# Scores of fifteen batches by seven block products in place of eight, in a transformer block on one core

## The chip, the cores and the metric

One of the eight cores of a Trainium2 chip runs the whole kernel. The metric is the device time of one execution in microseconds (us), the median of three runs. A profiled execution of its own gives the trace: for each engine every instruction with its start and length, and who released it. TensorE does the matmuls, VectorE (DVE), ScalarE (ACT) and GpSimd (POOL) the element work, SyncE (SP) issues nearly all transfers. A "bank" is one of the eight banks of PSUM (512 columns of float32 on 128 partitions).

## The reference

Sixteen batches of 1024 rows with 256 columns go through attention and a gated feed-forward part:

```python
def attn(t, W_qkv, b_qkv):
    qkv = jnp.einsum('bnd,ed->bne', t, W_qkv) + b_qkv
    Q, K, V = qkv[:, :, :256], qkv[:, :, 256:512], qkv[:, :, 512:]
    scores = jnp.einsum('bqd,bkd->bqk', Q, K) / jnp.sqrt(jnp.float32(256))
    return jnp.einsum('bqk,bkv->bqv', jax.nn.softmax(scores, axis=-1), V)

def ffn(x, w_gate, w_up, w_down):        # int32 weights times 1/127, hidden size 768
    gate = jnp.einsum('bsd,hd->bsh', x, wg)
    up = jnp.einsum('bsd,hd->bsh', x, wu)
    return jnp.einsum('bsh,dh->bsd', jax.nn.silu(gate) * up, wd)

x = x + layernorm(attn(layernorm(x), W_qkv, b_qkv))
x = x + layernorm(ffn(layernorm(x), w_gate, w_up, w_down))
```

## The kernel before

Every float32 operand of a matmul is split into a high and a low half of 16 bits (names ending in h and l), and a product a x b is three matmuls: high x high, high x low, low x high (`pairs`, `passes`, line 710). A batch has eight tiles of 128 rows; `g` is the half of four tiles, `b` the batch.

The steps of a batch. `x_stats`, `x_norm`, `x_hat`, `x_high` and `x_low` normalise x into `xs` and split it into `xh`, `xl`; `turn_x` transposes these by DMA into `xTh`, `xTl`. `project_z` multiplies with the folded matrix A = Wq'Wk, so that the scores are z times x transposed; `z_high` (ScalarE), `z_float` (VectorE) and `z_low` (GpSimd) split z from PSUM. `score(b, i)` makes the 128 x 1024 scores of query tile i in two banks: per bank 2 x 3 matmuls of 512 columns, one group of three for each half `dj` of the 256 columns that are summed over. `row_max` (L613, L617) takes the row maximum and makes the bias `nmx`, `exp` (L438) makes P, which frees the two banks; `p_high` and `p_low` split P, `turn_p` transposes it. `attend(b, g, u)` multiplies P with x (12 matmuls of 512 columns; four of them per half `g`, two for each output half `dh`), `o_high` and `o_low` split the result, `project_v` applies V (24 matmuls of 256 columns). `y_scale`, `y_stats`, `y_norm`, `x1_add` make the first residual in `X[k]`, `x1_norm`, `y_hat`, `y_high`, `y_low`, `turn_y` its normalised transposed halves `yTh`, `yTl`. `gate_up(b, g, c)` makes one of six hidden chunks of gate and up in two banks (8 matmuls of 512 columns, since the low half of the integer weights is zero here), `silu` (L473), `h_mul` (L679), `h_high` (L480) and `h_low` (L374) make its halves, `down` (24 matmuls of 256 columns) the output, `d_stats`, `d_norm`, `d_add`, `add_bias` the second residual, and `store` writes it. `reload` loads x a second time into one of four slots of `X`.

Nothing schedules this at run time. The order on each engine is written out by hand: a start-up part, a loop over the batches (on TensorE from b = 1 to 12), and the last batches. A wait is a semaphore and a count (`wait_ge`); a `gate_up` or `score` names in its call the semaphores that say its two banks are free. On TensorE a pass of the loop is: attends of batch b with scores of b + 1 between them, then the twelve `gate_up` of batch b, with `project_z` of b + 2 and the `down` of b - 1 and b between them. `attend` of batch b uses the banks 6 and 7, `project_v` and `down` 4 and 5, scores 0 to 3, and gates and z take 0 to 3, 6 and 7 in turn.

## Time and the profile before

| | |
|---|---|
| median of 3 runs | 1382.4 us (1381.77 to 1383.32) |
| the profiled execution | 1381.28 us, its span from first to last instruction 1379.5 us |
| TensorE busy | 1347.5 us (98%), 7332 matmuls |
| VectorE, ScalarE, GpSimd busy | 897.7, 879.5, 826.1 us |
| mean granted clock | 0.997 of full speed |

The page of the profile lists busy time by engine, the span in 40 slices, the DMA queues, the chain that ended last and the costliest groups. Matmuls overlap in the array, so their mean length (380 ns for 512 columns) is longer than the distance from one to the next.

### The profile page before, as it was taken

What the parts mean: (1) busy time and instruction counts of PE and PEld (TensorE: products, weight loads), DVE (VectorE), ACT (ScalarE), POOL (GpSimd) and SP (SyncE); (2) the same over time, 40 slices, a digit from 0 to 9 for tenths busy, and PEclk for the clock granted to TensorE, in tenths of its full rate; (3) what the DMA queues carried; (4) which work ended last, traced back from release to release, by engine and by line L of the source; (5) the groups of instructions that cost most, each with busy time, mean ns of one, the idle gap of its engine ahead of it and who ended that gap; (6) DMA issues with size and microseconds to landing.
All of it is one profiled execution on the core that took longest, in us unless ns stands there. A gap on an engine that the chain in (4) does not pass through costs nothing.

```text
span 1379.5 us, 22219 instructions
## 1 busy us (share of the span) xinstructions
PE 1347.5 (98%) x7332; PEld 721.1 (52%) x7332; DVE 897.7 (65%) x2160; ACT 879.5 (64%) x1373; POOL 826.1 (60%) x1002
## 2 busy tenths in 40 slices
PE   6898999999999999999999999999999999999987
PEld 3353555554555545555554555545555555555544
DVE  5875666666657667666666656667566666657565
ACT  4757575675766567575775757567575774756544
POOL 1768376484746748376484755748376484745544
PEclk9999999999999999999999999999999999999999
DMA  6997382653827457383653736547373664716311
GB/s 191 175 186 166 55 160 68 138 133 69 161 77 130 115 96 141 88 154 73 134 142 69 161 78 122 123 92 146 79 151 85 121 135 82 136 56 121 92 36 51
DMA packets 437175, 158.27 MB, mean 115 GB/s; under 512 B 418113, under 2 KB 420417, under 8 KB 437058
## 3 DMA queue, kind: packets, MB, share of 16 engines
q1 hardware_dynamic: 436272, 156.03, 54.5%
q8 instruction: 60, 0.98, 0.3%
q10 hardware_dynamic: 786, 0.79, 0.2%
q14 instruction: 57, 0.47, 0.1%
HBM read 36.70 MB, written 16.78 MB: 39 GB/s over the span
## 4 chain that ended last, share of the span: by engine, by line
PE 94%; DVE 3%; issue 1%; DMA 1%; POOL 1%; ACT 0%; ACTq 0%; POOLq 0%
PE S L710 93%; DMA hTh<-in_L_attn_W_qkv 1%; DVE mxs L613 0%; DVE S L642 0%; DVE st L651 0%; POOL rs L293 0%; PE S L736 0%; DMA yTl<-yl 0%; DVE st L669 0%; DVE X L664 0%; DVE hf L679 0%; DVE zw L606 0%; POOL yl L365 0%; DVE xl L320 0%; ACT yn L458 0%
## 5 line engine op out<-in xcount | busy, mean ns | idle before, releaser
L438 ACT ACTIVATE P<-S,nmx,sc 128x1024 f32<-128x1024 f32 x128 | 154.0, 1203 | 282.5 <-DVE nmx L617 282.5
L613 DVE TENSOR_REDUCE mxs<-S 128x1 f32<-128x1024 f32 x128 | 156.2, 1220 | 125.0 <-PE S L710 124.7
L679 DVE SCALAR_TENSOR_TENSOR hf<-S,sc,hf 128x512 f32<-128x512 f32 x192 | 142.0, 746 | 140.1 <-ACT hf L473 134.3
L338 POOL TENSOR_TENSOR Pl<-P,Ph 128x1024 f16<-128x1024 f32 x96 | 206.0, 2147 | 33.9 <-issue 26.4
L710 PE MATMUL S<-xTh,zTh 128*128 128x512 f16 x512 | 194.6, 380 | 4.4 <-ACT P L438 2.2
L710 PE MATMUL S<-PTh,xh 128*128 128x512 f16 x512 | 194.0, 379 | 1.0 <-DVE hf L679 1.0
L710 PE MATMUL S<-xTh,zTl 128*128 128x512 f16 x512 | 194.8, 380 | 0.0
L710 PE MATMUL S<-xTl,zTh 128*128 128x512 f16 x512 | 194.7, 380 | 0.0
L710 PE MATMUL S<-PTl,xh 128*128 128x512 f16 x512 | 194.0, 379 | 0.0
L710 PE MATMUL S<-PTh,xl 128*128 128x512 f16 x512 | 194.0, 379 | 0.0
L289 POOL TENSOR_SCALAR rs<-mv,sc 128x2 f32<-128x2 f32 (+1 forms) x96 | 35.3, 368 | 230.7 <-DVE mv L655 191.3
L710 PE MATMUL S<-Wh,hTh 128*128 128x256 f16 x768 | 170.4, 273 | 1.9 <-DVE X L703 1.7
L374 POOL TENSOR_TENSOR hTl<-hf,hTh 128x512 f16<-128x512 f32 x128 | 146.3, 1157 | 41.1 <-ACT hTh L480 36.8
L710 PE MATMUL S<-Wh,hTl 128*128 128x256 f16 x768 | 170.4, 273 | 0.0
L473 ACT ACTIVATE hf<-S,sc 128x512 f32<-128x512 f32 x192 | 130.9, 683 | 54.2 <-POOL hTl L374 35.6
L293 POOL TENSOR_TENSOR rs<-rs,mhalf 128x4 f32<-128x4 f32 (+1 forms) x160 | 145.2, 907 | 13.3
L710 PE MATMUL S<-yTh,Gh 128*128 128x512 f16 x384 | 146.1, 380 | 5.3 <-DMA yTl<-yl 3.9
L710 PE MATMUL S<-yTl,Gh 128*128 128x512 f16 x384 | 146.0, 380 | 0.0
L710 PE MATMUL S<-yTh,Uh 128*128 128x512 f16 x384 | 146.0, 380 | 0.0
L710 PE MATMUL S<-yTl,Uh 128*128 128x512 f16 x384 | 146.0, 380 | 0.0
L480 ACT ACTIVATE hTh<-hf 128x512 f16<-128x512 f32 x192 | 120.0, 625 | 34.3 <-DVE hf L679 34.3
L445 ACT ACTIVATE Ph<-P 128x1024 f16<-128x1024 f32 x128 | 135.3, 1057 | 5.2 <-DMA PTl<-Pl 1.7
(113 smaller groups left out, 2462.2 us busy)
## 6 DMA issues: line engine op xcount, KB each, us to landing
xs<-in_L_attn_t SPq DMA_DIRECT2D x32, 512.0 KB, 5.3
X<-in_L_attn_t SPq DMA_DIRECT2D x32, 512.0 KB, 4.6
out_x<-X SPq DMA_DIRECT2D x64, 256.0 KB, 2.9
PTh<-Ph SPq DMA_TRANSPOSE x128, 3.2
PTl<-Pl SPq DMA_TRANSPOSE x128, 3.3
hTh<-in_L_attn_W_qkv ACTq DMA_DIRECT2D x1, 768.0 KB, 7.2
hTl<-in_L_ffn_w_gate SPq DMA_DIRECT2D x1, 768.0 KB, 7.2
hTh<-in_L_ffn_w_up SPq DMA_DIRECT2D x1, 768.0 KB, 9.0
```

Of the source, the lines that this page charges most:

```text
L289: p.engine.tensor_scalar(rs, var, scalar1=eps, scalar2=mul, op0=ALU.add, **({} if mul is None else {"op1": ALU.mult})).then_inc(g_step, 1)
L293: return p.engine.tensor_tensor(out=rs, in0=rs, in1=mhalf[:, 0:rs.shape[1]], op=ALU.pow)
L338: p.engine.tensor_tensor(out=Pl[:, m % 3, :], in0=P[:, m % 2, :], in1=Ph[:, m % 3, :], op=ALU.subtract).then_inc(pl_vector if i in PL_ON_V ...
L374: p.engine.tensor_tensor(out=hTl[g][:, c, :], in0=hf[:, n % 3, :], in1=hTh[g][:, c, :], op=ALU.subtract).then_inc(hl_vector if c in HL_ON_ ...
L438: a.engine.activation(P[:, m % 2, :], ps[:, bank:bank + 2, :].rearrange("p a n -> p (a n)"), ACT.Exp, bias=nmx[:, c:c + 1], scale=sS, accu ...
L445: a.engine.activation(Ph[:, m % 3, :], P[:, m % 2, :], ACT.Copy).then_inc(ph_done, 1)
L473: a.engine.activation(hf[:, n % 3, :], ps[:, bank, :], ACT.Silu, scale=sc2[:, 3:4]).then_inc(silu_done, 1)
L480: a.engine.activation(hTh[g][:, c, :], hf[:, n % 3, :], ACT.Copy).then_inc(hh_done, 1)
L613: v.engine.tensor_reduce(mxs[:, c:c + 1], ps[:, bank:bank + 2, :].rearrange("p a n -> p (a n)"), axis=AX.X, op=ALU.max, negate=True).then_ ...
L679: v.engine.scalar_tensor_tensor(out=hf[:, n % 3, :], in0=ps[:, bank + 1, :], scalar=sc2[:, 4:5], in1=hf[:, n % 3, :], op0=ALU.mult, op1=AL ...
L710: done = t.engine.matmul(out, s, m, start=(start and i == 0), stop=(stop and i == len(terms) - 1))
```

## The change

The scores of batch 0 stay as they are. For batches 1 to 15 the product z x' is cut in blocks, two by two by two: the rows of z into even and odd tiles (a pair j of tiles 2j and 2j + 1), the 256 summed columns into two halves, the keys into two halves. With z blocks A11, A12 (even tile), A21, A22 (odd tile) and x blocks B, sums on both sides are formed first (S1 to S4 of z in `z_mix`, T1 to T4 of x in `x_mix`, in place in `xs`), split into halves and, for x, transposed (`T_high`, `T_low`, `turn_T`). Seven products P1 to P7 and sums of them give the four blocks C11, C12 (even tile), C21, C22 (odd tile). Some of the sums are made by accumulating a product onto one that lies in the bank (P5 and then P3 onto P1 in bank 1, P7 and then P4 onto P6 in bank 2), others by VectorE with a copy of the earlier state that ScalarE took (`s1`, `s6`, `s15`). The VectorE sum also yields the maximum, which takes the place of `row_max`.

The order on all engines is new. In a pass of the loop on TensorE the `gate_up` of the second half of batch b - 1 and the first half of batch b follow the attention of batch b, so gates run half a batch later than before, and `project_z` and the scores of b + 2 (pairs 0 and 1) stand in the same pass. `X` has three slots in place of four. Scale constants change to leave room for the sums, the float staging buffer `ft` goes, and the three loads of feed-forward weights are issued earlier.

```diff
-        X = two("X", [128, 4, D], f32, 4)
+        X = two("X", [128, 4, D], f32, 3)
+        Th, Tl = two("Th", [128, 4, D]), two("Tl", [128, 4, D])
+        TTh, TTl = sb("TTh", [128, NT, 2, 128], f16), sb("TTl", [128, NT, 2, 128], f16)
+        s1, s6, s15 = sb("s1", [128, 512]), sb("s6", [128, 512]), sb("s15", [128, 512])
...
+        def T_high(a, b, g):
+            a.wait_ge(xm_done, 4 * (b - 1) + 4 - g)
+            a.wait_ge(T_turned[g], 32 * (b - 1))
+            a.engine.activation(Th[g][:, :, :], xs[:, 4 * g:4 * g + 4, :], ACT.Copy).then_inc(Th_done, 1)
...
+        def zm_high(a, b, g):
+            n, js = 2 * (b - 1) + g, slice(2 * g, 2 * g + 2)
+            z_used(a, b - 1, g)
+            for k in range(2):
+                a.wait_ge(zm_done, 4 * n + 2 * k + 2)
+                a.engine.activation(zTh[:, 3 + 2 * k:5 + 2 * k, js, :], zs[:, 2 * k:2 * k + 2, :, :], ACT.Copy).then_inc(zmh_done, 1)
+
+        def copy_P1(a, b, j):
+            n = 4 * (b - 1) + j
+            a.wait_ge(P1_done, n + 1)
+            a.wait_ge(C11_done, n)
+            a.wait_ge(C21_done, n)
+            a.engine.activation(s1[:, :], ps[:, 1, :], ACT.Copy).then_inc(s1_done, 1)
...
+        def x_mix(v, b, part):
+
+            xl_wait(v, b, 0)
+            xl_wait(v, b, 1)
+            x00, x01, x10, x11 = (xs[:, 4 * g:4 * g + 4, 128 * d:128 * d + 128] for g in range(2) for d in range(2))
+            for k, (out, x, y) in enumerate(((x00, x10, x00), (x10, x11, x10), (x11, x11, x00), (x01, x01, x11))):
+                if k // 2 == part:
+                    v.wait_ge(xm_done, 4 * (b - 1) + k)
+                    v.engine.tensor_tensor(out=out, in0=x, in1=y, op=ALU.subtract).then_inc(xm_done, 1)
...
+        def z_mix(v, b, g):
...
+            v.engine.tensor_tensor(out=S3, in0=A11, in1=A21, op=ALU.subtract).then_inc(zm_done, 1)
+            v.engine.tensor_tensor(out=S1, in0=A21, in1=A22, op=ALU.add).then_inc(zm_done, 1)
+            v.wait_ge(zm_done, 4 * n + 2)
+            v.engine.tensor_tensor(out=S2, in0=S1, in1=A11, op=ALU.subtract).then_inc(zm_done, 1)
+            v.wait_ge(zm_done, 4 * n + 3)
+            v.engine.tensor_tensor(out=S4, in0=A12, in1=S2, op=ALU.subtract).then_inc(zm_done, 1)
+
+        def add_max(v, out, a, s, seed, top):
+            return v.engine.tensor_tensor_reduce(out=out, in0=a, in1=s, scale=1.0, scalar=seed, op0=ALU.add, op1=ALU.max,
+                                                 accum_out=top)
...
+        def join_C22(v, b, j):
+            n = 4 * (b - 1) + j
+            v.wait_ge(P7_done, n + 1)
+            v.wait_ge(s15_done, n + 1)
+            add_max(v, ps[:, 3, :], ps[:, 2, :], s15[:, :], LOWEST, mxs[:, n % 2, 2:3]).then_inc(C22_done, 1)
+
+        def join_C12(v, b, j):
+            n = 4 * (b - 1) + j
+            v.wait_ge(P3_done, n + 1)
+            v.wait_ge(s6_done, n + 1)
+            v.wait_ge(C11_done, n + 1)
+            add_max(v, ps[:, 1, :], ps[:, 1, :], s6[:, :], mxs[:, n % 2, 0:1], mxs[:, n % 2, 1:2]).then_inc(C12_done, 1)
+            v.wait_ge(C12_done, n + 1)
+            nmx_of(v, 8 * b + 2 * j, mxs[:, n % 2, 1:2])
...
+        def product(t, bank, j, k, moving, start):
+            mh, ml = moving
+            done = None
+            for i, (s_, m) in enumerate(pairs((zTh[:, k, j, :], zTl[:, k, j, :], mh, ml))):
+                done = t.engine.matmul(cols(ps[:, bank, :]), s_, m, start=(start and i == 0), stop=(i == 2),
+                                       skip_group_check=not start)
+            return done
...
+        def score_first(t, b, j, free0, free1, free2, free3):
...
+            t.wait_ge(*free1)
+            product(t, 1, j, 0, x_block(b, 0, 0), True).then_inc(P1_done, 1)
+            t.wait_ge(*free2)
+            product(t, 2, j, 5, T_block(1, 1), True).then_inc(P6_done, 1)
+            t.wait_ge(*free0)
+            product(t, 0, j, 1, x_block(b, 0, 1), True).then_inc(P2_done, 1)
+            t.wait_ge(s1_done, n + 1)
+            product(t, 1, j, 4, T_block(0, 0), False).then_inc(P5_done, 1)
+            t.wait_ge(s6_done, n + 1)
+            t.wait_ge(*free3)
+            product(t, 2, j, 3, T_block(1, 0), False).then_inc(P7_done, 1)
+
+        def score_second(t, b, j):
+            n = 4 * (b - 1) + j
+            t.wait_ge(s15_done, n + 1)
+            product(t, 1, j, 6, x_block(b, 1, 1), False).then_inc(P3_done, 1)
+            t.wait_ge(C22_done, n + 1)
+            product(t, 2, j, 2, T_block(0, 1), False).then_inc(P4_done, 1)
...
+            for b in range(1, 14):
                 attend(t, b, 0, 1)
+                score_first(t, b + 1, 2, (exp_done, 8 * b + 11), (exp_done, 8 * b + 11), (exp_done, 8 * b + 12), (exp_done, 8 * b + 12))
                 project_v(t, b, 0, (ft_done[0], 4 * b - 2), (ft_done[1], 4 * b - 2))
                 attend(t, b, 1, 2, (ol_done[1], 2 * b + 1))
                 attend(t, b, 1, 3)
+                score_second(t, b + 1, 2)
                 attend(t, b, 1, 0, (ol_done[0], 2 * b + 1))
                 attend(t, b, 1, 1)
+                score_first(t, b + 1, 3, (exp_done, 8 * b + 13), (exp_done, 8 * b + 13), (exp_done, 8 * b + 14), (exp_done, 8 * b + 14))
+                score_second(t, b + 1, 3)
                 project_v(t, b, 1, (x1_done, 8 * b + 2), (x1_done, 8 * b + 4))
+                gate_up(t, b - 1, 1, 0, 6, (ol_done[0], 2 * b + 2), (ol_done[1], 2 * b + 2), three)
+                gate_up(t, b - 1, 1, 1, 0, (exp_done, 8 * b + 15), (exp_done, 8 * b + 15), three)
+                project_z(t, b + 2, 0, 2, (exp_done, 8 * b + 16), (exp_done, 8 * b + 16))
...
+                project_z(t, b + 2, 1, 0, (silu_done, 12 * b + 4), (hmul_done, 12 * b + 4))
+                attend(t, b + 1, 0, 2, (hmul_done, 12 * b + 6))
+                score_first(t, b + 2, 0, (zw_done, 4 * b + 11), (zw_done, 4 * b + 12), (silu_done, 12 * b + 5), (hmul_done, 12 * b + 5))
                 down(t, b, 0, 0, (ft_done[0], 4 * b), three)
+                score_second(t, b + 2, 0)
                 down(t, b, 0, 1, (ft_done[1], 4 * b), three)
+                attend(t, b + 1, 0, 3)
+                score_first(t, b + 2, 1, (exp_done, 8 * b + 17), (exp_done, 8 * b + 17), (exp_done, 8 * b + 18), (exp_done, 8 * b + 18))
+                score_second(t, b + 2, 1)
+                attend(t, b + 1, 0, 0, (silu_done, 12 * b + 6))
```

In the elided stretch of the loop stand the other ten `gate_up` (four more of batch b - 1, six of batch b) and the two `down(b - 1, 1, ...)`, the first of them behind eight `gate_up` and one `project_z`. VectorE's order around a pair j = 1 or 3 is `join_C11`, `o_low`, `join_C22`, `join_C12`, `join_C21`; for batch 15 the attends of each half are followed at once by `project_v`.

## Rows read from the trace of the kernel before

**Rows 1.** The page's first part: busy us, share of the span, instructions.

```profile
PE 1347.5 (98%) x7332; PEld 721.1 (52%) x7332; DVE 897.7 (65%) x2160; ACT 879.5 (64%) x1373; POOL 826.1 (60%) x1002
```

**Rows 2.** The chain that ended last, in order: start us, length us, what.

```profile
119.73 1150.22 PE S L710 x6312
```

**Rows 3.** Timeline of TensorE: start us, length us, engine, line, operation.

```profile
122.22 0.38 PE L710 MATMUL S<-yTl,Gh 128*128 128x512 f16 x1
122.44 0.38 PE L710 MATMUL S<-yTh,Uh 128*128 128x512 f16 x1
...
137.98 0.27 PE L710 MATMUL S<-Wh,hTh 128*128 128x256 f16 x1
138.09 0.27 PE L710 MATMUL S<-Wh,hTl 128*128 128x256 f16 x1
```

**Rows 4.** One batch: PE, PEld, DVE, ACT, POOL busy; clock, DMA share, GB/s.

```profile
460.00:543.00 83.00, 83.00 (x458) 44.57 (x457) 54.61 (x133) 54.56 (x87) 51.51 (x63) 1.00 0.59 115
```

**Rows 5.** Groups by line and shape: busy us, mean ns, idle us before and releasers.

```profile
L613 DVE TENSOR_REDUCE mxs<-S 128x1 f32<-128x1024 f32 x128 | 156.2, 1220 | 125.0 <-PE S L710 124.7 <-issue 0.3
L438 ACT ACTIVATE P<-S,nmx,sc 128x1024 f32<-128x1024 f32 x128 | 154.0, 1203 | 282.5 <-DVE nmx L617 282.5
L374 POOL TENSOR_TENSOR hTl<-hf,hTh 128x512 f16<-128x512 f32 x128 | 146.3, 1157 | 41.1 <-ACT hTh L480 36.8 <-DVE hf L679 4.3
...
L679 DVE SCALAR_TENSOR_TENSOR hf<-S,sc,hf 128x512 f32<-128x512 f32 x192 | 142.0, 746 | 140.1 <-ACT hf L473 134.3 <-PE S L710 5.7
L445 ACT ACTIVATE Ph<-P 128x1024 f16<-128x1024 f32 x128 | 135.3, 1057 | 5.2 <-DMA PTl<-Pl 1.7
L473 ACT ACTIVATE hf<-S,sc 128x512 f32<-128x512 f32 x192 | 130.9, 683 | 54.2 <-POOL hTl L374 35.6 <-PE S L710 18.2
...
L328 POOL TENSOR_TENSOR zTl<-zw,zTh 128x512 f16<-128x512 f32 x60 | 80.9, 1368 | 1.2 <-PE S L710 1.2
...
L320 POOL TENSOR_TENSOR xl<-xs,xh 128x1024 f16<-128x1024 f32 x30 | 63.8, 2127 | 0.0
...
L651 DVE BATCH_NORM_STATS2 st<-S 128x6 f32<-128x256 f32 x128 | 47.9, 416 | 0.0
...
L630 DVE SCALAR_TENSOR_TENSOR oTl<-S,oTh 128x512 f16<-128x512 f32 x64 | 44.0, 688 | 58.2 <-ACT oTh L451 57.9
...
L451 ACT ACTIVATE oTh<-S 128x512 f16<-128x512 f32 x64 | 37.5, 586 | 55.0 <-PE S L710 55.0
...
L438 ACT ACTIVATION_READ_ACCUMULATOR P<-S,nmx,sc 128x1 f32 x128 | 24.6, 192 | 0.0
```

**Rows 6.** The chain again, from 27 to 39 us: reader after TensorE, TensorE after writer.

```profile
27.85 2.76 PE S L710 x12
...
30.63 1.24 DVE mxs L613
...
35.34 0.75 DVE zw L606
...
36.14 2.76 PE S L710 x12
```

**Rows 7.** Timeline of TensorE around its stalls; in brackets idle time and releaser.

```profile
106.00 0.39 PE L710 MATMUL S<-xTh,zTh 128*128 128x512 f16 x1 [2.19 <-ACT P L438]
...
108.50 0.63 PE L710 MATMUL S<-xTh,zTl 128*128 128x512 f16 x1
108.92 0.63 PE L710 MATMUL S<-xTh,zTh 128*128 128x512 f16 x1
...
1280.51 0.38 PE L710 MATMUL S<-PTh,xh 128*128 128x512 f16 x1 [0.98 <-DVE hf L679]
...
1332.28 0.59 PE L710 MATMUL S<-yTh,Gh 128*128 128x512 f16 x1 [3.93 <-DMA yTl<-yl]
```

**Rows 8.** DMA from 40 to 60 us: queue share, and transposes' time to landing.

```profile
q1 hardware_dynamic: 11824, 3.91, 95.4%
...
xTl<-xl SPq DMA_TRANSPOSE x2, 3.2
```

More of the change, by code:

```diff
@@ new lines, in _ @@
+            copy_P15(a, 15, 1)
+            p_high(a, 15, 1)
+            y_hat(a, 13, 1, 0)
+            exp(a, 15, 2, 0)
+            y_hat(a, 13, 1, 1)
+            exp(a, 15, 3, 2)
+            p_high(a, 15, 2)
+            o_high(a, 14, 0, 0)
+            copy_P1(a, 15, 2)
+            copy_P6(a, 15, 2)
+            y_high(a, 13, 1)
+            copy_P15(a, 15, 2)
+            add_bias(a, 13, 0, 0)
+            p_high(a, 15, 3)
+            add_bias(a, 13, 0, 1)
+            o_high(a, 14, 1, 1)
@@ new lines, in _ @@
+            exp(a, 15, 4, 0)
+            exp(a, 15, 5, 2)
+            p_high(a, 15, 4)
+            p_high(a, 15, 5)
+            copy_P1(a, 15, 3)
+            copy_P6(a, 15, 3)
+            o_high(a, 14, 1, 0)
+            copy_P15(a, 15, 3)
+            y_hat(a, 14, 0, 0)
+            y_hat(a, 14, 0, 1)
+            exp(a, 15, 6, 0)
+            exp(a, 15, 7, 2)
+            y_high(a, 14, 0)
+            silu(a, 13, 1, 0, 6)
+            silu(a, 13, 1, 1, 0)
+            silu(a, 13, 1, 2, 2)
@@ L1397, in _ @@
-            y_high(a, 14, 0)
-            o_high(a, 14, 1, 1)
-            exp(a, 15, 5, 2)
-            p_high(a, 15, 5)
-            exp(a, 15, 6, 0)
-            p_high(a, 15, 6)
             silu(a, 14, 0, 0, 6)
```

1764 lines of the change are left out of this document (976 added, 788 removed).

## The prediction

> **What bounds the kernel now.** I read the page first: TensorE is busy 98% of the span, the other three compute engines 60 to 65% [rows 1]. Busy matmuls overlap, so the share alone proves little; the chain of waits, in order of time, does. From 119.7 us it holds nothing but matmuls for 1150.2 us [rows 2]. The timeline then gives what a matmul costs in that stretch: one of 512 columns starts 0.216 us after the one before it, one of 256 columns 0.109 us [rows 3]. Counting the source, the kernel has 4,992 of the first kind and 2,304 of the second behind the set-up: 1077.3 + 251.4 = 1328.7 us of the 1379.5. So the middle is a TensorE stream without a hole, and the 51 us left lie ahead of the first product, in the stalls before 121 us, and in the last 110 us. A matmul taken from the middle is worth its 0.216 us, as long as no other engine is then too slow. The view of equal stretches shows one batch as 83.0 us, with VectorE at 54.6, ScalarE 54.6 and GpSimd 51.5, at full granted clock [rows 4].
>
> **Removed.** Scores take eight block products per pair of query tiles; batches 1 to 15 now take seven. A product is three matmuls of 512 columns; 15 batches x 4 pairs x 3 = 180 matmuls fewer, 180 x 0.216 = **38.8 us** off the stream. Nothing else on TensorE changes in count (512-column products have the same shape as now).
>
> **Added to the others, per batch.** VectorE loses eight row maxima (1.22 us each) and gets sixteen joins. No row shows a join (add two tensors, keep the maximum). Nearest is the 512-column operation with one operand in PSUM, 0.75 us; 0.69 is the lowest of that size, 1.22 (a reduction of 1024 columns) what it would be at half the rate. I take 0.75, since it does the same reads. Eight sums of 256 columns in z_mix (0.42, as the statistics of 256 columns; at most 0.69) and four of 512 in x_mix (0.69, as o_low, the shortest row of 512 columns with two tensors; at most twice that, since here both operands lie in SBUF and no row has both in float32). 54.6 - 9.8 + 12.0 + 3.4 + 2.8 = 63.0 us. ScalarE: twelve copies out of PSUM at 0.59, two T_high at 1.06, four zm_high of 512 columns at 0.68, z_high in six pieces of about 0.5 for four of 0.68 (an estimate from the 512-column row: half the columns, most of the fixed part): 54.6 + 7.1 + 2.1 + 2.7 + 0.3 = 66.8. GpSimd: two T_low at 2.13, four zm_low at 1.37, z_low in smaller pieces (about -1.3): 60.0 [rows 4, 5]. All are under the 81 us that TensorE will want, so each addition costs nothing by its sum; what counts is order and latency. The four turn_T per batch land in 3.2 us like other transposes, and the queues are half empty in the middle [rows 4, 8].
>
> **The new chain inside a pair of tiles.** TensorE now waits for copies of its own results. A group of twelve starts at 27.85 and its reader at 30.63; 12 x 0.216 = 2.59 is the group's share of the stream, so a reader starts 0.19 us after a product's share has passed. z_float ends at 36.09 and TensorE goes on at 36.14, 0.05 us after a writer [rows 6]. Count from P1's start, with a product 0.65: P6, P2, P5 and P7 start at 0.65, 1.29, 1.94, 2.59. The copy of P1 ends at 0.65 + 0.19 + 0.59 = 1.43, before 1.94; the copy of P6 before 2.59. P5's copy ends at 2.59 + 0.19 + 0.59 = 3.37, and P3 could have started at 3.24: 0.18 lost. C22 starts when P7 is visible (3.43), ends at 4.18, and P4 could have started at 4.07: 0.16 lost. VectorE has o_low (0.69) between C11 and C22 in both such pairs, which puts C22 about 0.15 later: **0.5 us a pair** where score_second stands right behind score_first. That is so for j = 1 and j = 3, two pairs in each of 15 batches: 15.0 us. Bounds: 0.34 each (10 us), and with joins of 1.22 us 0.5 + 0.47 (29 us). For j = 0 a down product (24 x 0.109 = 2.6 us) stands between, for j = 2 a project_v and two attends (7.8 us); those hide the chain. The bank releases are covered too: the exp of both tiles ends some 3.5 us behind P4 (0.19, a join, a bias of some 0.2, two exps of 1.2 and a read of 0.19), and two 12-matmul groups (5.2 us) stand between a pair and the next.
>
> One tight place more: P1 of j = 0 goes into a bank that z_float has to free. After project_z: 0.19, a third of z_high, z_float, z_high, z_float = 2.5 us, behind an attend of 2.59. And ScalarE's copy of P1 there stands behind add_bias, which waits for d_add behind z_float: ready at about 4.55 where P5 wants it at 4.53. I give 0.25 us a batch to both, 3.5 us in 14 batches; without the cover of that attend it would be 2.5 us a batch.
>
> The accumulator deserves a doubt. On ScalarE a result kept beside an output is a second instruction of 0.19 us [rows 5]. The Trainium skill (VectorE: DVE Perf Modes, section on two Vector instructions with no wait between them) counts a VectorE operation that also writes its accumulator as two instructions; the trace before has no such VectorE operation. If the read costs what ScalarE's does, each immediate pair loses 0.19 more, 5.7 us in all; I leave it out of the sum and inside the range.
>
> **Start.** Now the stream loses, up to 119.7 us, 2.35 us for an exp (a gap of 2.19 and a start late), 1.7 us because the clock is granted at half (1.2 of 2.4 GHz) for eight matmuls (0.42 us apart where 0.216 is full rate), 0.3, and 1.45 for a bank that z_float frees, which ends where the long stretch begins: 5.8 us [rows 2, 7]. After the change gate_up(0,0,0) needs y of the first half. Counted from P1 of the last pair of batch 1, ScalarE has: copies to 3.4, x_high and p_high 2.1, four y_hat 2.1, an exp with its read 1.4, y_high 1.06; GpSimd y_low 2.13; the transpose 3.2: 15.4 us. TensorE has the pair (5.0), project_v 2.6, project_z 2.6: 10.2. It stalls 5.2 us, and the clock falls as it did after the gap of 2.19 us: 1.7 more. z_low of batch 0 in three pieces costs 0.6. Together 7.5, so **+1.7 us**.
>
> **End.** The gap of 3.93 us for y goes (six gate_up of batch 14 and more now stand ahead), with its half clock, 4.08 + 1.7, and 1.14 us around a gap of 0.98: 6.9. But project_v(15, g) now follows the last attend at once: 0.19 + 0.59 + 0.69 + 0.05 = 1.5 us for o_high and o_low, twice: 3.0. **-3.9 us** [rows 5, 7]. The stall before the last down stays.
>
> **Gates half a batch later; three slots of X.** The order matters where gates release banks. Count from the start of gate_up(b-1,1,0). GpSimd waits for y_stats (3.7 us by the four y_scale and eight statistics operations of 0.42 and less), then y_norm 1.8 (four small operations), y_low 2.1, two h_low 2.3, x_low 2.1, z_low 2.1, two h_low 2.3: 16.4. down(b-1,1,0) stands behind eight gate_up (1.73 each) and a project_z, at 16.4, and needs chunks 3 to 5 at 17.0. That is 0.6 us of margin, so I cost it at nothing, though narrowly. The third X slot is reloaded behind stores that end a dozen microseconds before x1_add asks: nothing.
>
> **Sum.** 1379.5 - 38.8 + 15.0 + 3.5 + 1.7 - 3.9 = 1357.0 us of span. The profiled execution took 1381.28, 1.8 more than its span; the median of the runs, 1382.4, is another 1.1 above: 1359.9, say **1360 us**.
>
> **Rivals.** (A) Joins at half rate: an immediate pair loses 0.47 more (14 us) and, with its accumulator, up to 0.66 (20 us), while VectorE's batch grows by 16 x 0.66 to 73.5 us and its order begins to bind, say 0.5 us a batch (7 us): with 18 us for the pairs 1385 us. For it: no such row; against: every 512-column row with a PSUM operand takes 0.69 to 0.75. By the Trainium skill (Vector Engine (DVE) Microarchitecture Reference, section 7) a scalar-tensor-tensor with two SBUF sources that are not bf16 halves its throughput for want of a port for the accumulator; here one source is in PSUM, and h_mul's row with the same sources is not halved.
> (B) The other side: the gates' half binds. One mechanism, GpSimd's h_low of chunk 4 in front of down(b-1,1,0). The margin is 0.6 us; each microsecond beyond it costs one per batch. The gain left above, 22.5 us, is gone at 1.6 us a batch, so GpSimd 2.2 us later than counted decides. At 3 us late the time is 1360 + 14 x 2.4 = 1394 us. For it: nine operations in a row, counted without any wait for ScalarE's halves, and silu waits for hTl already, 35.6 us in all [rows 5]; against: the middle today has no hole.
> (C) The chain is hidden: shorter latencies, stalls half as long, and no y stall at the start: 1345 us.
> (D) The start is bound by transposes: from 40 to 60 us the queues are 95% busy [rows 8], and turn_T adds four of 1.3 us and batch 1's need comes earlier: up to 10 us, 1370 us.
>
> **Numbers.** Forecast 0.56 (its own range 1350 to 1368), A 0.10, B 0.10, C 0.12, D 0.12. This kernel's measurement can tell about 0.2%, 2.8 us. Faster by more: forecast, C, D and a little of A and B, 0.82; within it 0.04; slower 0.14. The range 1346 to 1383 leaves out the lower half of C and most of A and B.
>
> **What would show it.** TensorE with 7,152 matmuls; between 121 and 1270 us holes of 0.1 to 0.3 us ahead of P3 (released by ScalarE's copy) and P4 (by the join), two of each per batch, and no half clock; a join at 0.75 us; the first gate waiting for yTl; no wait of 3.9 us at the end. I am wrong if joins take over 1 us, if TensorE waits for hTl or hf in the gates, or if holes exceed 1.5 us a batch.

## The result and the profile after

The changed kernel took 1486.99 us (median of four runs, 1486.27 to 1487.63) where the kernel before took 1382.09 (1381.41 to 1383.32): a ratio of 1.0758, 95% interval 1.0743 to 1.0772. It is 105 us slower; 1360 was forecast, 22 us faster. Both the sign and the size were wrong, and the range missed by 104 us.

First the page's busy times, which answer to [rows 1]:

```profile
PE 1355.5 (91%) x7152; PEld 705.2 (47%) x7152; DVE 1180.7 (79%) x2703; ACT 1047.1 (70%) x1683; POOL 978.4 (66%) x1084
```

The 180 matmuls are gone, as foretold, but TensorE is no longer busy throughout. The page's chain that ended last, by engine and by line, had been one stretch of matmuls for 1150 us [rows 2]:

```profile
PE 56%; DVE 24%; issue 10%; POOL 3%; ACT 3%; DMA 2%; SPq 2%; DVEq 0%; ACTq 0%; POOLq 0%
PE S L854 45%; PE S L935 11%; DVE zs L708 3%; DVE hTl L419 3%; DVE zs L710 2%; DVE hf L823 2%; DVE xs L688 2%; DVE zs L707 2%; DMA xTl<-xl 2%; SPq L277 1%; DVE st L674 1%; DVE S L715 1%; DVE zw L698 1%; DVE X L847 1%; POOL Tl L353 1%
```

A quarter of it is VectorE, at the lines of z_mix (zs), x_mix (xs), its own h_low (hTl) and h_mul (hf). The joins (S L715) are 1%. One batch, from one project_z to that of the next batch, in the columns of [rows 4]:

```profile
206.90:296.40 89.50, 83.72 (x446) 43.50 (x444) 73.56 (x171) 66.22 (x108) 62.59 (x69) 0.98 0.58 118
```

89.5 us where 80.4 would be the bare stream (83.0 less 12 matmuls). ScalarE is at 66.2 (66.8 forecast), GpSimd at 62.6 (60.0), but VectorE at 73.6 where 63.0 was forecast. The groups by line and shape say which of its operations (columns as in [rows 5]; L707 to L712 are z_mix, L688 x_mix, L419 h_low, L715 the joins, here those with a seed, and the read of their accumulator):

```profile
L715 DVE CUSTOM_DVE_ANT_0 S<-S,s,mxs 128x512 f32<-128x512 f32 x120 | 90.5, 754 | 1.1 <-PE S L935 0.6
...
L688 DVE TENSOR_TENSOR xs<-xs 128x512 f32<-128x512 f32 x60 | 75.9, 1265 | 2.4 <-POOL xl L346 1.4
L419 DVE TENSOR_TENSOR hTl<-hf,hTh 128x512 f16<-128x512 f32 x64 | 74.8, 1168 | 9.0 <-ACT hTh L559 8.6
...
L712 DVE TENSOR_TENSOR zs<-zw,zs 128x256 f32<-128x256 f32 x30 | 47.9, 1598 | 1.0
...
L708 DVE TENSOR_TENSOR zs<-zw 128x256 f32<-128x256 f32 x30 | 46.6, 1552 | 0.0
...
L710 DVE TENSOR_TENSOR zs<-zs,zw 128x256 f32<-128x256 f32 x30 | 36.1, 1202 | 1.0
...
L715 DVE DVE_READ_ACCUMULATOR2_ANT mxs<- 128x1 f32 x240 | 34.0, 142 | 0.0
...
L707 DVE TENSOR_TENSOR zs<-zw 128x256 f32<-128x256 f32 x30 | 25.7, 856 | 0.1
```

A z_mix operation was priced at 0.42 us and takes 1.30 on average (156.3 us for 120), an x_mix operation 1.27 for 0.69. Shapes alone can't explain 0.86 beside 1.60 us for the same 256 columns. The timeline of VectorE over some microseconds of a batch, and below it GpSimd's, can:

```profile
212.20 0.50 DVE L707 TENSOR_TENSOR zs<-zw 128x256 f32<-128x256 f32 x1
212.63 1.38 DVE L708 TENSOR_TENSOR zs<-zw 128x256 f32<-128x256 f32 x1
214.04 2.24 DVE L710 TENSOR_TENSOR zs<-zs,zw 128x256 f32<-128x256 f32 x1
216.31 1.26 DVE L712 TENSOR_TENSOR zs<-zw,zs 128x256 f32<-128x256 f32 x1
...
218.57 2.06 DVE L823 SCALAR_TENSOR_TENSOR hf<-S,sc,hf 128x512 f32<-128x512 f32 x3
220.55 2.83 DVE L688 TENSOR_TENSOR xs<-xs 128x512 f32<-128x512 f32 x2
```

GpSimd's:

```profile
211.26 2.45 POOL L419 TENSOR_TENSOR hTl<-hf,hTh 128x512 f16<-128x512 f32 x2
213.68 2.31 POOL L346 TENSOR_TENSOR xl<-xs,xh 128x1024 f16<-128x1024 f32 x1
215.95 1.34 POOL L361 TENSOR_TENSOR zTl<-zw,zTh 128x512 f16<-128x512 f32 x1
```

Read the ends: L710 ends at 216.28, just behind GpSimd's xl (215.99); L708 at 214.01, just behind GpSimd's second hTl (213.71); L712 at 217.57, behind zTl (217.29). One VectorE operation of two SBUF sources ends a moment after each GpSimd operation ends, however short it would be by itself. The h_mul between them, which have a source in PSUM, did not lengthen: 742 ns on average over all 192, 746 before [rows 5].

What TensorE makes of it, in its timeline of the same batch:

```profile
219.36 0.39 PE L854 MATMUL S<-yTh,Uh 128*128 128x512 f16 x1 [1.91 <-DVE hf L823]
...
225.09 0.27 PE L854 MATMUL S<-Wh,hTh 128*128 128x256 f16 x1 [2.30 <-DVE hTl L419]
...
226.26 0.42 PE L854 MATMUL S<-Wh,hTh 128*128 128x256 f16 x1
226.47 0.42 PE L854 MATMUL S<-Wh,hTl 128*128 128x256 f16 x1
...
251.41 0.39 PE L935 MATMUL S<-TTh,zTh 128*128 128x512 f16 x1 [1.12 <-DVE mxs L715]
...
260.30 0.38 PE L935 MATMUL S<-TTh,zTl 128*128 128x512 f16 x1
260.72 0.39 PE L935 MATMUL S<-xTh,zTh 128*128 128x512 f16 x1
```

The wait of 1.91 us is for a bank that h_mul frees, behind z_mix in VectorE's order; the 2.30 us are for down's hTl, behind x_mix; then the clock is granted at half (matmuls of 256 columns 0.21 us apart from 225.6 to 228.4, 0.11 at full rate [rows 3]), 1.7 us; the 1.12 us are for C22, since z_mix of the second half ended late in front of the joins. The half clock is no accident of this batch: between 150 us and the last project_z it is granted in 13 stretches, and what the matmuls there lose by starting at twice their distance adds up to some 20 us of the middle. At 260 us stands the first of the two holes that were forecast in a pair: 0.42 us between starts where 0.22 is the stream, 0.20 ahead of P3; the one ahead of P4 is 0.24.

All of TensorE in one table: the distances of its matmuls' starts less 0.216 us for 512 columns and 0.109 for 256, added up. "Start" runs from the first project_z to 150 us, "middle" to the last project_z (13 batches in the changed kernels), "end" to the last matmul.

```
                      first z    start   middle    end
before                19.7 us     14.6      0.3    9.3
after                 21.3        41.2    117.5    8.7
```

1.6 + 26.6 + 117.2 - 0.6 - 38.8 = 106.0 us; the spans differ by 106.3.

### The profile page after: what moved, and what is told of

Same layout as the page of the kernel before. It is cut to its first block, busy times and chain, and to the rows that moved or that the text cites. A ratio compares the mean times of both kernels' runs of the same rounds, so it can differ in the third digit from the quotient of the medians.

```text
span 1485.8 us, 23358 instructions
## 1 busy us (share of the span) xinstructions
PE 1355.5 (91%) x7152; PEld 705.2 (47%) x7152; DVE 1180.7 (79%) x2703; ACT 1047.1 (70%) x1683; POOL 978.4 (66%) x1084
## 4 chain that ended last, share of the span: by engine, by line
PE 56%; DVE 24%; issue 10%; POOL 3%; ACT 3%; DMA 2%; SPq 2%; DVEq 0%; ACTq 0%; POOLq 0%
PE S L854 45%; PE S L935 11%; DVE zs L708 3%; DVE hTl L419 3%; DVE zs L710 2%; DVE hf L823 2%; DVE xs L688 2%; DVE zs L707 2%; DMA xTl<-xl 2%; SPq L277 1%; DVE st L674 1%; DVE S L715 1%; DVE zw L698 1%; DVE X L847 1%; POOL Tl L353 1%
## 5 line engine op out<-in xcount | busy, mean ns | idle before, releaser
L854 PE MATMUL S<-Wh,hTh 128*128 128x256 f16 x768 | 189.5, 290 | 33.5 <-DVE hTl L419 31.7
L419 POOL TENSOR_TENSOR hTl<-hf,hTh 128x512 f16<-128x512 f32 x128 | 159.9, 1269 | 73.9 <-ACT hTh L559 38.3
L854 PE MATMUL S<-Wh,hTl 128*128 128x256 f16 x768 | 189.5, 290 | 0.0
L823 DVE SCALAR_TENSOR_TENSOR hf<-S,sc,hf 128x512 f32<-128x512 f32 x192 | 137.6, 742 | 24.0 <-PE S L854 14.4
L715 DVE CUSTOM_DVE_ANT_0 S<-S,s 128x512 f32<-128x512 f32 x120 | 83.9, 700 | 55.6 <-PE S L935 41.5
L935 PE MATMUL S<-TTh,zTh 128*128 128x512 f16 x240 | 91.9, 383 | 17.4 <-DVE mxs L715 14.9
L321 POOL TENSOR_SCALAR rs<-mv,sc 128x2 f32<-128x2 f32 (+1 forms) x96 | 29.0, 302 | 118.2 <-DVE mv L795 90.3
L854 PEld LDWEIGHTS S<-Wh,hTh 128*128 128x128 f16 x768 | 79.5, 104 | 57.0 <-issue 34.9
L321 POOL TENSOR_SCALAR rs<-mv 128x4 f32<-128x4 f32 x64 | 25.5, 398 | 117.6 <-DVE mv L817 82.7
```

The costliest lines, as they stand in the source:

```text
L321: p.engine.tensor_scalar(rs, var, scalar1=eps, scalar2=mul, op0=ALU.add, **({} if mul is None else {"op1": ALU.mult})).then_inc(g_step, 1)
L419: p.engine.tensor_tensor(out=hTl[g][:, c, :], in0=hf[:, n % 3, :], in1=hTh[g][:, c, :], op=ALU.subtract).then_inc(hl_vector if c in HL_ON_ ...
L715: return v.engine.tensor_tensor_reduce(out=out, in0=a, in1=s, scale=1.0, scalar=seed, op0=ALU.add, op1=ALU.max, accum_out=top)
L823: v.engine.scalar_tensor_tensor(out=hf[:, n % 3, :], in0=ps[:, bank + 1, :], scalar=sc2[:, 4:5], in1=hf[:, n % 3, :], op0=ALU.mult, op1=AL ...
L854: done = t.engine.matmul(out, s, m, start=(start and i == 0), stop=(stop and i == len(terms) - 1))
L935: done = t.engine.matmul(cols(ps[:, bank, :]), s_, m, start=(start and i == 0), stop=(i == 2), skip_group_check=not start)
```

## The experiments

Each kernel is the changed one with the edit shown, but for the two ports programs. Where one run is named, there is one timed execution and no interval; elsewhere the median of four runs is given, with the ratio to the kernel before and its 95% interval in brackets. Middle and start are counted as in the table above.

### Is it the sums' form, or GpSimd beside them?

**ports.** A program of its own, which does none of the kernel's work: VectorE does eight operations of each kind, each waiting for the last, first alone, then while GpSimd subtracts 1024 columns without pause.

```diff
+ for n in range(70): p.tensor_tensor(out=pc[n % 4][:, :], in0=pa[:, :], in1=pb[:, :], op=ALU.subtract)
+ for _ in range(8): step(v.tensor_tensor(out=ra[:, 0:256], in0=u[:, 0:256], in1=w[:, 0:256], op=ALU.subtract))
```

> A kernel of its own, which leaves out the whole computation and times VectorE operations alone and then while GpSimd runs subtractions of 1024 columns back to back. Theory PORT (a VectorE operation with two SBUF tensors can only run between two GpSimd operations): a subtraction of 256 columns with both operands in SBUF takes 0.42 us alone and about 2.1 us beside GpSimd, one of 512 columns 0.68 and 2.1, even one of a single column about 2; with one operand in PSUM it stays near 0.45. Theory FORM (two float32 operands in SBUF are slow in themselves): 0.8 us or more for 256 columns alone, and the same beside GpSimd.

Measured, VectorE's timeline, alone and then beside GpSimd (length of eight):

```profile
3.10 3.65 DVE L65 TENSOR_TENSOR ra<-u,w 128x256 f32<-128x256 f32 x8
...
18.41 3.63 DVE L71 TENSOR_TENSOR rd<-S,w 128x256 f32<-128x256 f32 x8
22.08 2.59 DVE L73 TENSOR_SCALAR re<-u 128x256 f32<-128x256 f32 x8
24.70 3.66 DVE L75 BATCH_NORM_STATS2 st<-u 128x6 f32<-128x256 f32 x8
...
31.53 1.52 DVE L79 TENSOR_TENSOR rg<-u,w 128x1 f32<-128x1 f32 x8
...
35.70 19.89 DVE L65 TENSOR_TENSOR ra<-u,w 128x256 f32<-128x256 f32 x8 [2.52 <-POOL pc L46]
...
99.55 3.63 DVE L71 TENSOR_TENSOR rd<-S,w 128x256 f32<-128x256 f32 x8
103.21 17.37 DVE L73 TENSOR_SCALAR re<-u 128x256 f32<-128x256 f32 x8
120.62 3.67 DVE L75 BATCH_NORM_STATS2 st<-u 128x6 f32<-128x256 f32 x8
...
127.45 18.33 DVE L79 TENSOR_TENSOR rg<-u,w 128x1 f32<-128x1 f32 x8
```

Two sources in SBUF: 0.46 us becomes 2.49. One of them in PSUM: 0.45 stays 0.45. A single column: 0.19 becomes 2.29. So nothing is shared by bandwidth; the operation waits its turn. GpSimd's operations start 2.48 us apart beside VectorE's of 256 columns and 2.30 us apart once VectorE is done: one VectorE operation gets through for each of GpSimd's. Alone the form costs 0.46 us for 256 columns and 0.72 for 512, close to the 0.42 and 0.69 of the prediction; FORM is out.

**z_one_column, z_memset, zx_memset.** In the kernel itself, in steps: z_mix on the first column of each block (the rest of zs is zero), z_mix as memsets of full size, x_mix as memsets too. The scores of batches 1 to 15 are then not the reference's.

```diff
-            S3, S1, S2, S4 = (zs[:, k, :, :] for k in range(4))
+            S3, S1, S2, S4 = (zs[:, k, :, 0:1] for k in range(4))          # z_one_column, and the A blocks alike
...
-            v.engine.tensor_tensor(out=S3, in0=A11, in1=A21, op=ALU.subtract).then_inc(zm_done, 1)
+            v.engine.memset(S3, 0.5).then_inc(zm_done, 1)                  # z_memset, and S1, S2, S4 alike
...
-                    v.engine.tensor_tensor(out=out, in0=x, in1=y, op=ALU.subtract).then_inc(xm_done, 1)
+                    v.engine.memset(out, 0.5).then_inc(xm_done, 1)         # zx_memset has both
```

> The changed kernel with the four sums of z_mix on one column of 128 in place of all (the scores are not the reference's). PORT: the wait for GpSimd's running operation stays, only the 0.25 us of columns go, eight times a batch: 1 to 2 us a batch at most, so 1460 to 1480 us. FORM: the cost goes with the columns, some 7 us a batch: 1385 to 1400 us.

> The changed kernel with the four sums of z_mix replaced by memsets of the same tiles, which read nothing (the sums are left out). PORT: z_mix falls from 5.2 to about 1.5 us a half, twice a batch, most of which is on the path through VectorE: 1400 to 1430 us. A theory CHAIN, by which the waits inside the pairs of tiles cost the time: 1480 us, no change.

> As the one before, with the four differences of x_mix replaced by memsets too (both kinds of sums left out, all their waits, copies, splits and transposes kept). PORT: nothing of the new VectorE work with two SBUF operands is left, the time comes to that of my forecast, 1355 to 1375 us. CHAIN, or GpSimd late with hTl (rival B): it stays above 1400 us.

Measured in one run each, 1425.66, 1414.76 and 1377.78 us, beside a kernel before of 1384.17; the middle is 62.8, 53.7 and 17.4 us. z_memset is in PORT's range, zx_memset 3 us above it and far below CHAIN's. z_one_column hit neither range. Two of its four groups show why it was too quick for PORT as I had put it and too slow for FORM:

```profile
L712 DVE TENSOR_TENSOR zs<-zs,zw 128x2 f32<-128x2 f32 x30 | 34.7, 1157 | 1.0
...
L710 DVE TENSOR_TENSOR zs<-zw 128x2 f32<-128x2 f32 x30 | 5.5, 183 | 0.0
```

Two elements a row still take 0.78 us on average over the four (93.4 us for 120), where one column took 0.19 undisturbed in ports: the waits stay. But the second of a set, L710, is 183 ns in the mean of all 30: it is short and needs no result of the first, and seems to get through with it. So a set of four waits less often than four times. In zx_memset VectorE is busy 63.4 us of a batch (73.6 in the changed kernel), and the batch takes 81.5:

```profile
300.00:381.50 81.50, 81.20 (x445) 42.95 (x444) 63.36 (x169) 65.42 (x107) 60.34 (x69) 1.00 0.66 130
```

That is the middle the prediction had: it forecast 1.25 us a batch above the stream, 16.3 in 13 batches, and 17.4 are there. In the batch read no hole over 0.3 us is left, and the clock is at full rate in the whole middle. VectorE's h_low still waits in this run (1.37 us on average, 1.17 in the changed kernel), and TensorE doesn't feel it. The run does not isolate waiting from length: a memset of 256 columns is 0.27 us, not 0.42. What it shows is that x_mix and z_mix carry 100 of the 117 us, the half clock behind their holes included; the chain in a pair and the new order, which are kept here, don't.

**yield.** All work is kept; only GpSimd is made to wait while VectorE forms sums.

```diff
+                p.wait_ge(zm_done, 8 * (b + 3) - 4)
                 x_low(p, b + 3, 1)
...
+                p.wait_ge(xm_done, 4 * (b + 3) - 2)
                 zm_low(p, b + 3, 0)
...
                 z_low(p, b + 3, 1)
+                p.wait_ge(zm_done, 8 * (b + 3))
                 p_low(p, b + 2, 7)
```

> All work is kept; GpSimd waits in batches 3 to 15 at three places until VectorE has formed the sums: ahead of x_low(b,1) for z_mix(b,0), ahead of zm_low(b,0) for x_mix(b,0), ahead of p_low(b-1,7) for z_mix(b,1). Theory PORT (a VectorE operation with two sources in SBUF gets through only between two GpSimd operations): the sums fall from 0.86 to 1.6 us each towards 0.43 and 0.69, the wait at C11 of pair 0 and the hTl gap shrink by 1 to 3 us a batch: 1440 to 1470 us, although GpSimd is given less time. Rival CHAIN (what the middle loses is latency and order, GpSimd's share is harmless): added waits only make h_low later, 1487 or above.

Measured 1441.70 us (1438.78 to 1442.87), ratio 1.0420 (1.0402 to 1.0437): adding three waits to an engine takes 45 us off. The middle falls from 117.5 to 69.8 us; some 15 of these 48 us are the clock, which is at half in 3 stretches of the middle in place of 13. VectorE's timeline at the same place of a batch, and below it GpSimd's:

```profile
470.68 1.39 DVE L707 TENSOR_TENSOR zs<-zw 128x256 f32<-128x256 f32 x1
471.99 0.41 DVE L708 TENSOR_TENSOR zs<-zw 128x256 f32<-128x256 f32 x1
...
472.90 0.42 DVE L712 TENSOR_TENSOR zs<-zw,zs 128x256 f32<-128x256 f32 x1
473.24 0.68 DVE L419 TENSOR_TENSOR hTl<-hf,hTh 128x512 f16<-128x512 f32 x1
```

GpSimd's:

```profile
469.52 2.27 POOL L419 TENSOR_TENSOR hTl<-hf,hTh 128x512 f16<-128x512 f32 x2
473.40 2.52 POOL L346 TENSOR_TENSOR xl<-xs,xh 128x1024 f16<-128x1024 f32 x1 [1.61 <-DVE zs L712]
```

With GpSimd idle from 471.8 to 473.4 the last three sums and h_low take 0.41, 0.42, 0.42 and 0.68 us, the very prices of the prediction. This is the clearest run for the cause: the same instructions, undisturbed. But it frees only part of the sums. In batches 3 to 15 z_mix takes 2.6 us in the first half (5.5 in the changed kernel) and 4.4 in the second (5.3), and x_mix 5.75 a batch, more than the 5.1 before: GpSimd has no idle time that x_mix ended, so the second of the three waits never held it up.

**x_mix_gpsimd.** x_mix of batches 3 to 15 moved to GpSimd.

```diff
-                x_mix(v, b + 3, 0)          # and part 1
...
                 h_low(p, b, 1, 4)
+                x_mix(p, b + 3, 0)
+                x_mix(p, b + 3, 1)
                 zm_low(p, b + 3, 0)
```

> All work is kept; the four subtractions of x_mix of batches 3 to 15 run on GpSimd, between h_low(b-3,1,4) and zm_low(b,0), in place of VectorE. Theory PORT: VectorE loses four operations of 1.27 us a batch and meets more GpSimd work with the rest; GpSimd gains four of some 1.2 us, in the stretch that feeds h_low and down. TensorE should wait less for hf and more for hTl: between 1465 and 1490 us. A theory in which VectorE's own speed at these operations is the fault (FORM, already weakened) would see 13 x 5 us x half of it on the path: 1450 or less.

Measured 1521.86 us, ratio 1.1006 (1.0988 to 1.1025): 32 us above the top of my range. Moved to GpSimd, the four operations take 1.38 us each there, and VectorE's rest gets worse (z_mix 1.43 us on average, h_low 1.44). VectorE's load fell (1149 us busy for 1181) and the kernel slowed, so VectorE's load is not what binds. GpSimd's rose (1032 for 978), and the waits aren't those I named: in the batch from 437.6 to 529.9 us down waits 0.3 us for hTl, but P1 of a pair waits 2.1 us for z_float, and P3 2.2 us for ScalarE's copy. Neither theory had foreseen the size.

### What sets how long a VectorE operation waits?

**ports_short, pool_halves, pool_quarters.** ports again with GpSimd's operations at 256 columns; then in the kernel GpSimd's steps of 1024 columns cut in two pieces of 512, or in four of 256 with h_low in two.

```diff
-            p.engine.tensor_tensor(out=yl[:, :, :], in0=yn[:, :, :], in1=yh[:, :, :], op=ALU.subtract).then_inc(yl_done, 1)
+            for i in range(parts):                    # x_low, T_low, p_low alike, on GpSimd alone
+                done = p.engine.tensor_tensor(out=out[:, i * w:i * w + w], in0=a[:, i * w:i * w + w],
+                                              in1=b[:, i * w:i * w + w], op=ALU.subtract)
```

> The run ports again, with GpSimd's operations of 256 columns (about 0.65 us) in place of 1024 (2.13 us). Theory GAP: a VectorE operation with sources in SBUF alone gets through once between two GpSimd operations, so its step shortens with them: about 0.45 + 0.6, that is 0.7 to 1.2 us for 256 columns, and 0.6 to 0.9 us for one of 1 column, where both were 2.3 to 2.5. Rival SHARE: the two engines share bandwidth in a fixed proportion whatever GpSimd's length; then 2.3 to 2.5 us again. Operations with a source in PSUM stay at 0.45 us by both.

> All work and every order are kept; GpSimd's operations of 1024 columns (x_low, T_low, y_low, p_low) are issued as two of 512, so that none of its operations is longer than 1.16 us. GpSimd itself gets some 1.5 us a batch more to do. Theory GAP (a VectorE operation with sources in SBUF alone waits for the end of GpSimd's running operation): the sums of x and z and VectorE's own h_low get shorter, by up to 1 us where they stood beside a long one: 1455 to 1480 us. Rival CHAIN or a mere lack of time on GpSimd: 1487 or more.

> As pool_halves, with pieces of 256 columns for the same four steps and for h_low: some 7 us a batch more on GpSimd (65.6 to about 72 of 89 us), and VectorE gets in after 0.65 us. GAP alone would give 1430 to 1465 us; but GpSimd's h_low is what down waits for, and each VectorE operation that gets in holds GpSimd up, so it may lose part or all of that again: above 1480 the added length of GpSimd's order counts for more.

ports_short, one run, VectorE's timeline beside GpSimd: eight operations of 256 columns took 6.96 us (0.87 each), of one column 5.31 (0.66), with a PSUM source 3.63 as ever.

```profile
34.07 6.96 DVE L65 TENSOR_TENSOR ra<-u,w 128x256 f32<-128x256 f32 x8 [0.91 <-POOL pc L46]
...
75.24 5.31 DVE L79 TENSOR_TENSOR rg<-u,w 128x1 f32<-128x1 f32 x8
```

GAP holds: the wait follows the length of GpSimd's single operation, though GpSimd is busy without pause in both. SHARE is out. In the kernel pool_halves took 1472.44 us (ratio 1.0646, 1.0628 to 1.0664), 14.5 less than the changed kernel with more instructions on GpSimd; pool_quarters 1478.10 (1.0688, 1.0670 to 1.0706), above its range. In pool_quarters the z sums fall further (0.84 us on average, 1.12 in pool_halves, 1.30 after) and the middle is the same (104.4 and 103.4 us). What VectorE gains is lost elsewhere. In the batch from 393 to 482 us of pool_quarters TensorE's hole for hf is gone and the one for C22 under half a microsecond, but one of about 4 us stands ahead of down, for GpSimd's h_low (2.3 in pool_halves, for VectorE's); behind it the clock is at half, for longer than in pool_halves in ten of 13 batches. The half clock costs some 30 us of the middle there and 17 in pool_halves.

### What is left in yield?

**yield_order, yield_order_start, yield_halves_start.** In yield's timeline of TensorE the first down of the gates' half still waits for h_low on GpSimd:

```profile
481.49 0.27 PE L854 MATMUL S<-Wh,hTh 128*128 128x256 f16 x1 [2.22 <-POOL hTl L419]
```

yield_order puts that h_low ahead of z_low (and zm_low of the other half ahead of two p_low); the others add the start of the next part, the last one with yield's own order and the halves.

```diff
+                p.wait_ge(zm_done, 8 * (b + 3) - 4)
                 x_low(p, b + 3, 1)
-                z_low(p, b + 3, 0)
                 h_low(p, b, 1, 3)
                 h_low(p, b, 1, 4)
+                z_low(p, b + 3, 0)
+                p.wait_ge(xm_done, 4 * (b + 3) - 2)
                 zm_low(p, b + 3, 0)
```

> As yield (1441.7 us), with GpSimd's order changed as well, in batches 3 to 15: h_low(b,1,3) and (b,1,4) now come ahead of z_low(b+3,0), and zm_low(b+3,1) ahead of p_low(b+2,6) and 7. In yield the first down of the gates' half still waits 2.2 us for hTl from GpSimd, whose two h_low stand behind 2.3 us of z_low. Theory: that wait goes, and the half clock behind it, some 2.5 to 3.5 us in each of 13 batches: 1396 to 1412 us. Rival: the two h_low now run beside x_mix, one VectorE operation gets through at each, and hf is late in place of hTl: 1430 to 1445.

> yield_order and start_all_orders together. If start and middle are separate, its time is that of yield_order less what start_all_orders gains (0 to 12 us): 1388 to 1412 us. It would have to be under 1379 to beat the kernel before; I do not expect that, since the sums still meet GpSimd's work in each batch.

> yield (1441.7 us), start_all_orders (-4 us) and pool_halves together. If what is left in yield's middle (70 us above the stream, where zx_memset had 17) is still VectorE's sums beside long GpSimd operations, the halves give 5 to 20 us more: 1417 to 1433 us. If it is GpSimd's lateness with h_low, nothing or worse: 1437 or more.

Measured 1451.63 us (1.0499, 1.0481 to 1.0516), 1448.15 and 1441.92 (1.0429, 1.0411 to 1.0446). yield_order is 10 us slower than yield, where 30 to 46 less were forecast: my theory of it fell, and yield_order_start missed its range with it. Its holes in a batch of over 0.5 us, in TensorE's timeline:

```profile
482.54 0.27 PE L854 MATMUL S<-Wh,hTh 128*128 128x256 f16 x1 [1.50 <-DVE hTl L419]
...
518.74 0.39 PE L935 MATMUL S<-TTh,zTh 128*128 128x512 f16 x1 [2.90 <-DVE mxs L715]
```

The wait at down is shorter by 0.7 us but now ends with VectorE's h_low, which stands behind x_mix beside GpSimd's work; and the wait for C22 grew to 2.9. That is the rival that the expectation named, in effect, though 7 us above its range: hTl of one engine late in place of the other's. It is slower although z_mix of the second half fell too, to 2.8 us: what a sum costs depends on who waits behind it. The halves, worth 14.5 us by themselves, give nothing beside the waits: yield_halves_start has a start of 35.0 us where yield has 42.6, and a middle of 76.0 where yield has 69.8. Of the 70 us left in yield's middle some 17 are the chain inside a pair and some 5 the half clock; x_mix still stands beside GpSimd's work; what divides the other 48 between contention and GpSimd's own lateness was not settled. No version tried beats the kernel before with its computation whole.

### The start

**start_order, start_all_orders, zx_memset_start.** The start lost 28 us where 1.7 was forecast. The first rows of TensorE's waits there:

```profile
52.13 0.59 PE L854 MATMUL S<-xTh,Ah 128*128 128x512 f16 x1 [5.14 <-ACT P L517]
...
60.00 1.44 PE L889 MATMUL S<-hf,am 128*1 128x128 f32 x6 [3.73 <-ACT P L517]
...
66.44 0.59 PE L896 MATMUL S<-pw,hf 1*128 1x6 f32 x2 [5.00 <-DVE pw L614]
...
134.42 0.61 PE L854 MATMUL S<-yTh,Gh 128*128 128x512 f16 x1 [3.99 <-DMA yTl<-yl]
```

start_order moves one VectorE step forward, the p_low for which ScalarE's exp waits 5.89 us; start_all_orders also ScalarE's p_high, z_high and exp ahead of T_high, GpSimd's p_low ahead of T_low, and the scale factors ahead of z_mix; zx_memset_start is zx_memset with start_order's move.

```diff
             row_max(v, 0, 3, 2)
+            p_low(v, 0, 1)
             ffn_max(v, 1)
...
             x_mix(v, 1, 0)
-            p_low(v, 0, 1)
```

> One line of VectorE's start-up order is moved: p_low(0,1) goes from behind x_mix(1,0) to right behind row_max(0,3), ahead of ffn_max(1). Theory ORDER: in the start, exp(0,3) waits 5.89 us for this p_low, and TensorE with it 5.14 us and then at half clock; the gap at z(1,0) shrinks to under 1.5 us, and 7 to 10 us come off: 1476 to 1480 us. Rival WEIGHTS (the start is late because the feed-forward weights are loaded ahead of W, and because of work that piles up on VectorE whatever its order): under 3 us, 1484 to 1487.

> All work is kept; the start-up order is moved on three engines, since start_order only moved its wait of 5.1 us to the next matmul (10.1 us, for the exp of tile 5). With p_low(0,1) moved as there, ScalarE now does p_high(0,3), p_high(0,4), z_high(1,0) and exp(0,5) ahead of the two T_high of batch 1, GpSimd p_low(0,3) ahead of T_low(1,1), VectorE the scale factors of the feed-forward weights ahead of z_mix(1,0). Theory ORDER: the start loses by what is put ahead of the exps of batch 0; the waits of 10.1 and 5.0 us fall under 5 us together: 1474 to 1480 us. Rival LOAD: the work of batch 1 added between 30 and 90 us (x_mix, T halves, copies, sums) is too much in any order; what is gained at 60 us is lost at 75 to 90: 1483 to 1488.

> z_mix and x_mix replaced by memsets on VectorE, as in zx_memset (1377.8 us), with the move of start_order too. The scores of batches 1 to 15 are then formed from constants. If the two causes are separate and together nearly all that was missed, the middle stays within 1 us of zx_memset's (17.4 us above the stream) and the start gives the same 7 to 10 us as in start_order: 1367 to 1371 us. If the start's loss comes from the same contention, zx_memset has it already and nothing more is gained: 1375 to 1378.

Measured 1486.48 us (1.0748, 1.0730 to 1.0766), 1482.85 (1.0723, 1.0705 to 1.0741) and 1376.03 (0.9952, 0.9935 to 0.9969). start_order moved its hole and took nothing:

```profile
60.90 1.44 PE L889 MATMUL S<-hf,am 128*1 128x128 f32 x6 [10.12 <-ACT P L517]
```

In its timeline of TensorE 5.14 us are gone at 52 and 10.1 stand at 60, for the exp of a later tile, behind T_high and a p_low of GpSimd. start_all_orders moved that one too (5.90 and 3.98 us there), and 3.3 us grew at 76; it took 4.1 us in all, at the edge of the rival LOAD's range. In zx_memset the same move gave 1.75 us, not the 7 to 10 of its expectation, and the kernel before differed by as much between the two measurements (1384.17 and 1382.59): in effect nothing, as its rival said. So the start is not late by one misplaced step. Of its 28 us, the sums account for about 9 (41.2 against 31.9 in zx_memset), orders for about 4 (36.8 in start_all_orders), the first product's lateness for 1.6 (W lands at 8.7 us where it landed at 7.2; that the earlier loads of the feed-forward weights cause it was not tried). If these add up, the other 13 or so are open; that it is the mere work of batch 1 among the exps of batch 0 was argued, not shown.

## Why the prediction was wrong

**The step that failed** is the price of z_mix and x_mix, and the sentence that each addition costs nothing by its sum while the engines stay under 81 us. I priced eight sums at 0.42 us and four at 0.69 with an upper bound of twice that for the four, 1.4 us, and 0.69 for the eight. Undisturbed they cost that (yield: 0.41, 0.42; ports: 0.46 and 0.72). Beside GpSimd they took 1.30 and 1.27 us on average, up to 2.35 and 2.54: 10.4 + 5.1 us a batch for 3.4 + 2.8. These 9.3 us are most of VectorE's 10.6 above forecast. Even so 73.6 is under 89.5: the load does not bind, its place does. z_mix stands ahead of three h_mul that free gate banks, x_mix ahead of the h_low that down wants, and z_mix of the second half ahead of C22.

The trace before had the warning, in rows of VectorE's timeline that I didn't draw on: its own h_low, two SBUF sources, twice within 8 us:

```profile
130.22 1.22 DVE L374 TENSOR_TENSOR hTl<-hf,hTh 128x512 f16<-128x512 f32 x1
...
138.36 0.68 DVE L374 TENSOR_TENSOR hTl<-hf,hTh 128x512 f16<-128x512 f32 x1
```

The same shape at 1.22 and 0.68 us, 0.92 on average over 64, when the groups with a PSUM source stay within 0.04 us of their mean. The first stands beside a run of GpSimd operations (129.73 to 132.45 us), the second where GpSimd is idle (137.92 to 139.37). I wrote that no row had both operands in SBUF in float32; these were near enough. The Trainium skill says it outright, and I had not weighed it: SBUF — State Buffer, section "SBUF: two separate sides", calls the pair of ports that VectorE and GpSimd share an exclusive lock, taken by a VectorE operation with two SBUF inputs or in a two-port mode, or by GpSimd's, for the whole instruction. The traces agree point by point: two SBUF sources wait, PSUM and bn_stats don't (3.66 and 3.67 us), one column waits as long as 256, and a tensor_scalar with one float32 source in SBUF waits too (0.32 becomes 2.17 us), though the trace doesn't show whether it ran in a two-port mode.

**Rival B** had the place and the sign (holes in the gates' half, ahead of down) and was given 0.10. Its engine and its size were wrong: VectorE's h_low and h_mul, not GpSimd's count, and 9.0 us a batch above the stream, not 2.4 + 1.25. In yield the wait at down is GpSimd's (2.22 us), so B's own mechanism does appear once VectorE's is less. Its argument against, that the middle before has no hole, was no argument: before, the only VectorE work with two SBUF sources between gates was h_low itself. **Rival A** falls: a join takes 0.70 or 0.75 us, with 0.14 for its accumulator's read, so 0.75 was about right and the doubt about the read too. P4 is released by that read, which ends only 0.05 us behind the join (261.51 and 261.56 us in the batch shown), so it costs a pair 0.05 and not 0.19. That VectorE's batch of 73.6 us equals the 73.5 of A is chance: A had it from the joins. **Rival C** falls too: a pair loses 0.44 us, not half of 0.5, and the stall for y stands. **Rival D** has no wait of its own: of the start's waits over 1 us only the one for yTl, which the sum had, ends with a transpose. **The chain in a pair**: 0.44 us measured for 0.5, and 17.4 for 16.3 in the whole middle once the sums are out of the way. **The stream**: 38.8 us, exact (180 matmuls, same spacing). **The start**: +1.7 forecast, +28 measured; I followed ScalarE behind the last pair of batch 1 and found its wait for yTl (3.99 us for 5.2), but counted nothing of what x_mix, T_high, T_low and the new copies put ahead of the exps of batch 0 at 45 to 90 us. **The end**: -3.9 forecast; the y gap went, and the hole for o_high and o_low came as counted, once for each half:

```profile
1411.78 0.27 PE L854 MATMUL S<-Vh,oTh 128*128 128x256 f16 x1 [1.46 <-ACT oTh L530]
```

but the sum of the end came to -0.6, since two holes for hTl, 1.08 and 1.74 us, and one of 0.69 stand there now.

The half clock was forecast to be absent in the middle; it stands about once a batch, in the batch read for 1.7 us behind the hole at down. In yield, where the hole at down is as long (2.2 us), the batch read at 467 to 553 us has full clock, so the length of that one hole does not decide it. The prediction had no term for it in the middle, where it costs some 20 us.

How much was ever there: zx_memset_start, with sums shorter than any real ones, is half a per cent faster than the kernel before, 7 us. The seven products save 39 us, their chain takes 17, and its start is 18 us later than before (31.0 for 14.6, and 1.5 for the first product), which leaves little even with undisturbed sums.
